# Cross attention of a two-layer decoder: operands interleaved over the partitions by fewer transfers, sums added where they stand

## What is computed

```
q = rmsnorm((x @ Wq).reshape(8, 256, 32, 16))
k = rmsnorm(k.reshape(8, 256, 32, 16))
attn = softmax(q . k / sqrt(16)) over 256 keys
out = attn @ v, heads side by side      # (8, 256, 512)
x = layer_norm(x + out)
```

## Time and profile before

| | us |
|---|---|
| median of 3 runs (2881.52 to 2881.8) | 2881.75 |
| profiled execution, time | 2876.47 |
| profiled execution, span of its core | 2874.4 |
| cross_heads in it: first transfer issued to first matmul of the next stage | 2158.27 to 2356.98 |
| PE busy in the span | 2202.7 (77%) |
| DVE / ACT / POOL busy in the span | 1650.6 / 1253.6 / 909.7 |

### The profile page before, as it was taken

One profiled execution on the slowest core, in us unless ns is written; L12 is line 12 of the kernel. 1 busy time (PEld: TensorE's weight loads), 2 busy tenths in 40 slices (PEclk: granted clock), 3 DMA queues, 4 the chain that ended last, 5 costly groups with the idle time before them and its releaser, 6 DMA issues. The chain is left out here.

```text
span 2874.4 us, 34832 instructions
## 1 busy us (share of the span) xinstructions
PE 2202.7 (77%) x12666; PEld 1425.6 (50%) x12666; DVE 1650.6 (57%) x2238; ACT 1253.6 (44%) x2061; POOL 909.7 (32%) x605
## 2 busy tenths in 40 slices
PE   2886854063889899888469999988975666999996
PEld 0465741022666666666336777754432223555552
DVE  5359865948667777777434554544445766611115
ACT  0013224543767677666332222235545645322225
POOL 1005442204357777777252333342100002300000
PEclk7987867585999999999789999999987878999998
DMA  3135663003468999999620000021338941100001
GB/s 134 59 94 187 216 223 132 0 12 137 170 223 241 254 254 255 256 255 250 168 99 1 1 0 0 0 103 44 95 91 146 180 91 58 33 1 0 0 0 58
DMA packets 135619, 324.75 MB, mean 113 GB/s; under 512 B 32049, under 2 KB 60209, under 8 KB 131890
## 3 DMA queue, kind: packets, MB, share of 16 engines
q1 hardware_dynamic: 114418, 272.05, 30.1%
q0 software_dynamic: 21056, 50.84, 9.0%
HBM read 226.74 MB, written 96.88 MB: 113 GB/s over the span
## 5 line engine op out<-in xcount | busy, mean ns | idle before, releaser
L1406 DVE SCALAR_TENSOR_TENSOR x_part<-x_group,x_scale,x_part 128x256 f32<-128x256 f32 x660 | 288.0, 477 | 144.6 <-ACT x_part L1348 139.1
L1295 PE MATMUL x_group<-x_xt,x_gu 128*128 128x256 f16 x2640 | 346.9, 275 | 1.8 <-DVE x_xt L1398 0.9
L1348 ACT ACTIVATE x_part<-x_group,x_scale 128x256 f32<-128x256 f32 x660 | 275.7, 470 | 123.3 <-PE x_group L1295 90.1
L1261 POOL TENSOR_TENSOR x_part<-x_part 128x512 f32<-128x512 f32 x165 | 235.2, 1429 | 197.0 <-DVE x_part L1406 197.0
L1295 PEld LDWEIGHTS x_group<-x_xt,x_gu 128*128 128x128 fp8e4 x2640 | 237.5, 98 | 85.7 <-issue 32.7
L1632 POOL TENSOR_TENSOR c_pt<-c_pt,const_tables 128x256 f32<-128x256 f32 x128 | 127.8, 1019 | 281.0 <-ACT c_pt L1740 280.7
L1312 PE MATMUL x_y_ps<-x_d_hi,x_h_hi 128*128 128x512 f32 x330 | 160.2, 485 | 68.8 <-DVE x_h_lo L1419 66.3
L159 PE MATMUL mean_n<-residual,const_tables 128*128 128x512 f32 x160 | 77.4, 635 | 146.2 <-PEq L733 103.5
L1252 POOL DMA_INDIRECT mixed_rows<-x_y,moe_rows x94 | 150.0, 1596 | 31.6 <-issue 20.9
L2380 POOL TENSOR_TENSOR f_w_lo<-aux,f_w_hi 128x1536 bf16<-128x1536 f32 x11 | 40.3, 3660 | 365.7 <-ACT f_w_hi L2347 365.7
L2193 ACT ACTIVATE z_pt<-z_s 128x1024 f32<-128x1024 f32 x128 | 119.7, 1063 | 68.0 <-PE z_s L2165 67.6
(11 more groups left out here) (334 smaller groups left out, 5537.9 us busy)
## 6 DMA issues: line engine op xcount, KB each, us to landing
x_d_hi<-down_hi SPq DMA_DIRECT2D x50, 768.0 KB
x_d_lo<-down_lo SPq DMA_DIRECT2D x50, 768.0 KB
x_gu<-codes_gu SPq DMA_DIRECT2D x50, 384.0 KB
p_w<-d_s SPq DMA_DIRECT2D x17, 768.0 KB, 9.4
down_hi<-p_hi SPq DMA_DIRECT2D x17, 768.0 KB, 4.6
down_lo<-p_lo SPq DMA_DIRECT2D x17, 768.0 KB, 6.4
aux<-ct SPq DMA_DIRECT2D x2, 4096.0 KB, 15.7
cross_values<-y_v_out SPq DMA_DIRECT2D x16, 512.0 KB, 3.0
```

Of the source, the lines that this page charges most:

```text
L1261: pool.tensor_tensor(x[:, 0, :, :], x[:, 0, :, :], x[:, 1, :, :], ALU.add).then_inc(summed, 1)
L1295: mm = pe.matmul(group_ps[s % 2][:, q, :], codes[:, q, col:col + P], xt[u][:, k, q, :], start=k == 0, stop=k == 1)
L1348: act.activation(part[n % PARTS][:, q, o % 2, :], group_ps[s % 2][:, q, :], ACT.Copy, scale=scale[v][:, o, q:q + 1]).then_inc(ev_act, 1)
L1406: dve.scalar_tensor_tensor(x, group_ps[s % 2][:, 2 + q, :], scale[v][:, o, 2 + q:3 + q], x, ALU.mult, ALU.add).then_inc(ev_dve, 1)
```

## The change

Three things change together.

1. **Residual in natural order.** `feature_order()` is now 0 to 127. The two loads of each packed weight go to every second partition (`slice(half, P, 2)`), and a table column `nib_shift`, copied into `g.shift` by one small DVE instruction at the program's start, takes the place of the old shifts by halves. Two unused tables go.
2. **Operands in seven transfers.** The copies are interleaved: partition 4 r + copy holds row r of the 32 rows of a plane, so one transfer takes 32 rows of 8 KB to every fourth partition (256 KB), 3 for k and 3 for q, and v comes in one transfer of 1 MB. Every fourth partition (copy 3) is never loaded; it is zeroed once in both buffers, `k_st` by POOL and `q_st` by DVE, and loads 0 and 1 wait for that. The score matmuls take 64 rows in place of 48.
3. **No bounce.** A round now takes the sums of heads such that `z_at` comes out in the residual's order: `values(u)` uses four pairs' exponentials, one head (o) of each. So a round needs four pairs before its first sums, `RING_P` is 8, and in PE's order the `values` stand later: the last of a batch comes behind the scores of pairs 0 to 3 of the next. DVE adds `z_at` to the residual at the end of each batch by two `scalar_tensor_tensor` of 128x1024, one for each o, the second waiting for the first, with the columns of `half16` as factors 0 and 1. `o_dram`, `back` and their semaphores go.

```diff
@@ feature_order @@
-    p = np.arange(P)
-    return 2 * (p % 64) + p // 64
+    return np.arange(P)
@@ sparse_select, vector @@
+            step(dve.tensor_copy(g.shift[:, 0:1], g.const("nib_shift")))
@@ Prepare.load (two places), feed_forward (one) @@
-            r = slice(64 * half, 64 * half + 64)
+            r = slice(half, P, 2)
@@ cross_project, vector @@
-                    x = proj[i % 4][:, :].rearrange("p (q o j d) -> p q o j d", o=2, j=4, d=HDX)
+                    x = proj[i % 4][:, :].rearrange("p (q j o d) -> p q j o d", o=2, j=4, d=HDX)
@@ cross_heads @@
-    PAIRS, RING_P, LAG_P = HX // 2, 6, 2
+    PAIRS, RING_P, LAG_P = HX // 2, 8, 2
@@ cross_heads, sync @@
-                for e in range(2):
-                    for copy in range(COPIES):
-                        rows = slice(64 * e + HDX * copy, 64 * e + HDX * copy + HDX)
...
-            def bounce(b):
...
+                else:
+                    sp.wait_ge(k_zeroed, b + 1)
+                    sp.wait_ge(q_zeroed, b + 1)
+                for copy in range(COPIES):
+                    for x, n, half in ((k_st, 0, copy % 2), (q_st, 1, copy // 2)):
+                        of = g.stack_dram[n][half, b].rearrange("r p s -> r (p s)")
+                        sp.dma_start(x[i][copy:P:4, :, :].rearrange("r p s -> r (p s)"), of).then_inc(loaded[i], 16)
+                sp.dma_start(v_st[i][:, :, :, :].rearrange("p k h d -> p k (h d)"),
+                             g.v_dram[2 * b:2 * b + 2].rearrange("k p n -> p k n")).then_inc(loaded[i], 16)
...
+        @block.gpsimd
+        def _(pool):
+            for i in range(2):
+                pool.memset(k_st[i][:, :, :], 0.0).then_inc(k_zeroed, 1)
@@ cross_heads, tensor @@
             def values(u):
-                b, four = u // 8, u % 8
-                pe.wait_ge(exped, 2 * u + 2)
-                if u % 2 == 0 and u >= 4:
-                    pe.wait_ge(at_ready, u // 2 - 1)
+                b, r, o = u // 8, u // 2, u % 2
+                pe.wait_ge(exped, 4 * r + 4)
+                if o == 0 and r >= 2:
+                    pe.wait_ge(at_ready, r - 1)
...
-            for n in range(N + LAG_P):
+            for n in range(N + 2 * LAG_P):
                 if n < N:
                     score(n)
-                if n >= LAG_P and (n - LAG_P) % 2 == 1:
-                    values((n - LAG_P) // 2)
+                m = n - LAG_P - 3
+                if m >= 0 and m % 4 in (0, 2) and m // 4 < 4 * B:
+                    values(m // 2)
@@ cross_heads, scalar @@
-                    act.wait_ge(summed, (n - RING_P) // 2 + 1)
+                    act.wait_ge(summed, 2 * ((n - RING_P) // 4) + 2)
@@ cross_heads, vector @@
-                dve.tensor_tensor(x, x, back[b % 3][:, :, :], ALU.add).then_inc(added, 1)
...
+                for o in range(2):
+                    dve.scalar_tensor_tensor(x, at[b % 2][:, :, o, :], half[:, o:o + 1], x, ALU.mult, ALU.add)\
+                       .then_inc(added, 1)
+                    dve.wait_ge(added, 2 * b + o + 1)
+
+            for i in range(2):
+                dve.memset(q_st[i][:, :, :], 0.0).then_inc(q_zeroed, 1)
             for r in range(4 * B):
                 divide(r)
-                if r % 4 == 1 and r >= 8:
-                    add(r // 4 - 2)
+                if r % 4 == 3:
+                    add(r // 4)
```

More of the change, by code:

```diff
@@ L77, in constants @@
     p = np.arange(P)
-    order = feature_order()
     put("ident", np.eye(P))
@@ L88, in constants @@
     put("blk16", (p[:, None] // 16 == p[None, :] // 16) / 16.0)
-    put("perm", p[:, None] == order[None, :])
-    put("den16", np.concatenate([np.arange(32) < 16, np.arange(32) >= 16])[None, :])
     e = np.arange(E_ROUTED)
@@ L2103, in cross_heads @@
         crossed, den, at = two("crossed", [P, S]), two("den", [P, S]), two("at", [P, C, 2, S])
-        back = [sb(f"back{i}", [P, C, S]) for i in range(3)]
         s_ps = [ctx.enter_context(nc.psum_tensor(f"z_s{i}", [P, 2, 2, S], F32)) for i in range(3)]
         out_ps = [ctx.enter_context(nc.psum_tensor(f"z_out{i}", [P, 2, S], F32)) for i in range(2)]
-        loaded, bounced = ([sem(f"{n}{i}") for i in range(2)] for n in ("loaded", "bounced"))
-        returned = [sem(f"returned{i}") for i in range(3)]
+        loaded = [sem(f"loaded{i}") for i in range(2)]
         half = g.const("half16")
-        scored, exped, summed, step_sem, shuffled, inverted, at_ready, added = (
-            sem(n) for n in ("scored", "exped", "summed", "step", "shuffled", "inverted", "at_ready", "added"))
-        LOAD = 16 * (4 * COPIES + 2)
+        k_zeroed, q_zeroed, scored, exped, summed, step_sem, shuffled, inverted, at_ready, added = (
+            sem(n) for n in ("k_zeroed", "q_zeroed", "scored", "exped", "summed", "step", "shuffled", "inverted", "at_ready",
+                             "added"))
+        LOAD = 16 * 7
         block = ctx.enter_context(nc.Block())
@@ L2120, in load @@
                     sp.wait_ge(summed, 8 * (b - 1))
-                for e in range(2):
-                    for copy in range(COPIES):
-                        rows = slice(64 * e + HDX * copy, 64 * e + HDX * copy + HDX)
-                        from_rows = slice(HDX * e, HDX * e + HDX)
-                        for x, n, half in ((k_st, 0, copy % 2), (q_st, 1, copy // 2)):
-                            of = g.stack_dram[n][half, b, from_rows].rearrange("r p s -> r (p s)")
-                            sp.dma_start(x[i][rows, :, :].rearrange("r p s -> r (p s)"), of).then_inc(loaded[i], 16)
-                for k in range(2):
-                    sp.dma_start(v_st[i][:, k, :, :].rearrange("p h d -> p (h d)"), g.v_dram[2 * b + k])\
-                      .then_inc(loaded[i], 16)
-            def bounce(b):
-                i = b % 2
-                sp.wait_ge(at_ready, 4 * b + 4)
-                to = g.o_dram[b].rearrange("(q o j d) s -> o j d q s", o=2, j=4, d=HDX)
-                for o in range(2):
-                    for j in range(4):
-                        row = 2 * HDX * j + HDX * o
-                        sp.dma_start(to[o, j], at[i][row:row + HDX, :, o, :]).then_inc(bounced[i], 16)
-                if b >= 3:
-                    sp.wait_ge(added, b - 2)
-                sp.wait_ge(bounced[i], 128 * (b // 2 + 1))
-                of = g.o_dram[b].rearrange("(c r o) s -> o r c s", r=64, o=2)
-                for o in range(2):
-                    sp.dma_start(back[b % 3][64 * o:64 * o + 64, :, :], of[o]).then_inc(returned[b % 3], 16)
+                else:
[7 more added lines that the diff above has]
+                             g.v_dram[2 * b:2 * b + 2].rearrange("k p n -> p k n")).then_inc(loaded[i], 16)
             load(0)
@@ L2163, in score @@
                     for e in range(2):
-                        rows = slice(64 * e, 64 * e + ROWS)
+                        rows = slice(64 * e, 64 * e + 64)
                         mm = pe.matmul(s_ps[n % 3][:, e, k, :], k_st[b % 2][rows, pair, k * P:(k + 1) * P],
@@ L2295, in _ @@
                 for half in range(2):
-                    sp.dma_start(raw[n % 2][64 * half:64 * half + 64, :], a["ffn"][:, n, :]).then_inc(landed[n % 2], 16)
+                    sp.dma_start(raw[n % 2][half:P:2, :], a["ffn"][:, n, :]).then_inc(landed[n % 2], 16)
                 sp.dma_start(scales[n % 2], a["ffn_s"][:, n, :].to_broadcast([P, SLICE])).then_inc(landed[n % 2], 16)
```

27 lines of the change are left out of this document (12 added, 15 removed).

## The result

| | before | changed | difference |
|---|---|---|---|
| median of the runs, us | 2881.75 (3 runs, 2881.52 to 2881.8) | 2853.02 (3 runs, 2850.71 to 2853.32) | -28.7 |
| profiled execution, time | 2876.47 | 2853.32 | -23.2 |
| its span | 2874.4 | 2851.5 | -22.9 |
| the stage in it | 206.1 | 181.7 | -24.4 |

The ratio is 0.9898, with an interval of 0.9876 to 0.9921; three kernels further down were timed on one chip, the changed one among them: 2849.98 against 2876.93, 0.9904 (0.9887 to 0.9921). The rest of the program took between 2663.5 and 2670.5 us in all kernels of this study, with no order to it; it was 1.5 us longer in the changed kernel than before. Two or three us between medians say little for that reason, and the stage is what is compared.

The account below looks back on a forecast made before the run. Late operand loads in a chain, 21.3 us a batch, were taken as the bound. 2183.1 + 32 x 3.91 + 20.8 + 8.4 = 2337.4 for 2356.66 gave -19.3: 2857.2 profiled, 2862.4 us median, range 2849 to 2874 (0.85).

Parts of the forecast that it names:

- forecast A: Main forecast for the whole change: loads hidden, DVE the bound, clock falls behind additions; 2859 to 2873 us, chance 0.62.
- rival B: TensorE's clock stays at full in the gaps behind additions: 8.4 us less, 2854 us, band 2850 to 2858, chance 0.24.
- the step from the profiled execution to the median: End of the sum: the median of the runs lies 5.3 us above the profiled execution, 2862.4 from 2857.2.
- wait for zeroing: Stage start: load 0 waits for POOL's memset of 128x4096, 3.51 us by its elements; cost 3.6 us.
- signs of being wrong: The forecast is wrong if a round exceeds 3.91 us or another stage moves by more than 2 us.
- Transfers: Loads of k and q at 250 GB/s: a load takes 11.3 us for 18.3, hidden if under 14.3.
- Rival C: Loads half hidden, lengthening each batch beyond 14.3 us: at 140 to 185 GB/s 2864 to 2882 us, chance 0.05.
- DVE as the next bound: Once the chain of loads goes, DVE is late next: 3.91 us a round, 18.2 a batch with additions.
- The clock: PE's 3.3 us gaps behind additions drop its clock to half, seven times 1.2: 8.4 us (0 to 14).
- Additions: Two a batch in DVE's line at 1.3 us each with the wait: 20.8 us in eight batches (19.6 to 24.4).
- The round trip: The sums' trip between batches cost nothing but traffic; at the end it cost DVE 8.76 us, now gained.

Follow-up runs that it names:

- e7: The changed kernel with one more 1 MB transfer in each load, to a buffer nothing reads: stage 183.8 us against 181.7, median 2853.3 us.
- e8: The changed kernel with two more 1 MB transfers in each load, to buffers nothing reads: stage 199.7 us against 181.7, median 2869.43 us.
- e9: The changed kernel with the additions of batches 0 to 6 on POOL instead of DVE: stage 159.9 us against 181.7, median 2828.74 us.
- e1: The kernel before with the seven transfers, zeroing and 64 rows alone, old order and round trip kept: stage 174.4 us against 206.1, median 2844.75 us.
- e6: The changed kernel with each 32-row transfer to 32 neighbouring partitions, for time only: stage 182.9 us against 181.7, median 2851.92 us (one run).
- e5: The changed kernel with each k and q transfer cut into two of 16 rows to every eighth partition: stage 183.6 us, median 2852.8 us (one run).
- e4: The changed kernel with each batch's two additions moved apart, behind rounds 0 and 2 of the next batch: stage 176.8 us, median 2844.56 us.

## Why the prediction held, step by step

It said 2862.4 us with 2849 to 2874, faster; 2853.0 was measured. Mechanism and direction are as forecast, and the gain was put 9.4 us too small. The range held, but forecast A's own band, 2859 to 2873, did not: the time lies in B's, 2850 to 2858. Of the 9.4, 3.9 are in the profiled time, 2857.2 forecast and 2853.3 measured: the stage's sum was 5.4 too long, and the rest of the program was 1.5 longer than before, where the sum had no change. The other 5.5 come from the step from the profiled execution to the median. It added 5.3, which is how far the profiled execution of before lay under its median; that of after lies 0.3 above its own. How a single profiled execution lies to its median is chance, and no run shows the 5.3 for the changed kernel.

| step | predicted | measured |
|---|---|---|
| load, us | 11.3, load 0 12.5 | load 0 11.5; load 2 10.9, from its first issue to v's landing, and hidden |
| wait for zeroing | 3.6 | 3.5 |
| first score | 2174.4 | 2174.26, in a stage that starts 1.0 later |
| first round behind it | 8.7 | 8.4 |
| 32 rounds | 3.91 each | 3.91 each |
| eight pairs of additions | 20.8 | 22.0 |
| clock | 8.4 | 3.2 |
| last addition's end | 2337.4 | 2333.0 |

Relative to the stage's start the first round came 1.5 us earlier, the additions cost 1.2 more and the clock 5.2 less: -5.4 together, and 1.0 for the later start makes the 4.4 between 2337.4 and 2333.0. Of the signs of being wrong, no round without additions and with its sums there in time takes more than 3.93 us.

**Transfers.** 250 GB/s was taken and 256 to 283 came; the claim that any load under 14.3 us is hidden was borne out from both sides by e7 and e8. That made the forecast safe where its least certain number stood: between 12.4 and 9.1 us a load nothing but load 0 depends on it. Rival C's upper end, 185 GB/s, does not follow from it: k and q at 185 make a load of 13.5 us, which is hidden, and 14.3 is reached at 169. Issuing a load took 4.3 us, not under 4, since a transfer took 0.63 and not 0.46; that cost nothing.

**DVE as the next bound.** Right, and e9 shows it by taking the additions away.

**The clock** is the mis-sized term: "1.2 x 7 = 8.4 us", where 3.2 were measured. Its mechanism is there at five of seven gaps. In the one batch where both sums ran at half clock throughout (restart at 2298.90, DVE's gap 1.08) the round came 1.16 late, near the 1.0 of the step. But the step took this worst case for all seven, against its own figure for the clock's return, 3.7 us behind the restart: the second sums start there after 1.93 + 1.03 = 3.0 us, so only 0.7 us of them run at half clock, and they are there after about 4.4 us, 0.5 late. That is near what came in three of the seven. Behind 2205.17 the clock was back after 3.5 us, the sums were there after 4.2 (2209.36) and the round was 0.58 late. In all, two gaps had no fall, and in four only a part of the round's sums ran at half clock. A second late round never came, since PE at full clock has 0.75 us a round to spare. The mean is 0.46 a gap, not 1.2.

The clock also fell later than the 1.3 to 1.8 us into a gap that the prediction read from the kernel before. In three of the five it fell only when PE was at work again; behind 2205.17 that was at about 2205.2 (the window from 2205 has a mean of 0.62), 3.6 us behind the last matmul. In the other two it fell 2.0 and 2.9 us into the gap. The warning that the prediction cites from the Trainium skill, "TensorE: Matmul & The Clock Gate", section "HAM oscillation", that such a loop starts every turn cold, held for five turns of seven. In size the result is at rival B's 2854, while B's reason, that the clock stays, is false: that the time came out in B's band is the clock term's size and the chance in the step to the median.

**Additions.** 1285 ns each, as taken; but a pair adds 2.76 to its round, not 2.6: 0.15 us of starts and waits.

**The round trip.** Its removal was entered as a gain at the end, and e1 shows 8.9 us for it. What the prediction did not say is that it is bought too dearly: 12.8 us more of additions, 2.0 of late sums and 1.1 of start. The sum had all these terms, and set against "transfers alone" it would have shown it.

## What to carry to other kernels

Where transfers keep all DMA engines busy at a low rate, look at how many partitions each reaches, not at its bytes: here 16 neighbours gave 118 GB/s, 32 neighbours 205 to 229, every fourth of 128 256 to 283. Once loads are hidden, count each instruction on the engine that is the next bound: a round trip through DRAM beside it cost nothing but the last one's 8.9 us, while an addition in its line cost its full length each time (1.1 to 1.2 us alone, 2.76 a pair). Price a change in parts, each against the others and not only against before, and look for an idle engine to take what the bounding one must not do.

## What the runs showed of the hardware

- One behind the other, issues took SP 0.42 us each for 16 or 32 rows to neighbouring partitions and 0.59 to 0.61 for rows to every fourth or eighth. The time of a row is not that transfer's alone: the same transfer of v took 0.58 behind the strided ones of the changed kernel and 0.43 behind the neighbouring ones of e6. With 128 KB pieces issuing is itself the bound (197 GB/s in e5).
- TensorE's clock fell at, or just behind, five of seven gaps of 3.5 us in either profiled execution of the changed kernel, and at some gaps of 1.95 us in e4, not at others; the length of the gap alone does not tell it. Which of them fall was not worked out.
- DVE zeroed 128x2048 words of 32 bits in 1.76 us, 0.86 ns a word, where the prediction's 2.6 us went by additions of f32 at 1.25 ns an element.
- POOL and DVE worked side by side in e9, POOL for 72.7 us of 124, and a round of DVE stayed at 3.91 us. The Trainium skill's page "SBUF — State Buffer", section "Who interferes with whom", says that an instruction of DVE with at most one input in SBUF, outside its two-port modes, does not contend with GpSimd. Three of a round's five instructions read `z_out`, which is in PSUM, each reads at most one array from SBUF, and the trace agrees.
